# Second attention: queries and keys staged from ScalarE's queue instead of SyncE's

## The reference, cut to what matters

```python
q = qkv[..., :2 * Hx].reshape(Bx, 2 * NQ, Sx, HD)
k = qkv[..., 2 * Hx:2 * Hx + G].reshape(Bx, NKV, Sx, HD)
...
scores = jnp.einsum('bhqd,bhkd->bhqk', q, k) / math.sqrt(HD)
scores = jnp.where(causal, scores, -jnp.inf)
aw = jax.nn.softmax(scores, axis=-1)
...
aw = aw[:, :, 0] - lam * aw[:, :, 1]
attn = jnp.einsum('bhqk,bhkd->bhqd', aw, v) * (1.0 - LAMBDA_INIT)
```

## Time and profile before

| | |
|---|---|
| median of 3 runs | 695.55 us (694.66 to 696.96) |
| profiled execution, its own time | 693.89 us |
| its span, first to last instruction | 692.1 us |
| loop of the second attention | about 243 to 493 us |
| busy over the span: PE, DVE, ACT, POOL | 524.8, 469.4, 305.6, 341.8 us |
| mean granted clock of PE | 0.844 of full speed |

### The profile page before, as it was taken

The page is one execution under the profiler, slowest core; times in us unless marked ns, Lnnn a source line. Parts: engine busy times, 40 slices in busy tenths (PEclk is TensorE's granted clock), DMA queues, the critical chain, the costliest instruction groups (busy, mean ns, idle before and its releaser), DMA issues. The chain is left out here.

```text
span 692.1 us, 12597 instructions
## 1 busy us (share of the span) xinstructions
PE 524.8 (76%) x3770; PEld 352.6 (51%) x3770; DVE 469.4 (68%) x1716; ACT 305.6 (44%) x498; POOL 341.8 (49%) x489
## 2 busy tenths in 40 slices
PE   6686363987046799999899899999816189999950
PEld 3336262987023234544344444444416179999950
DVE  5958855554483897989799979995675734544535
ACT  3213011543016136767577667778411044445422
POOL 2050323777364425655467646855431067777622
PEclk9798855999558558999899989999965589999985
DMA  5000430111216434455654434433065011111122
GB/s 193 0 1 0 186 150 19 52 55 47 68 31 127 90 90 98 104 112 111 137 138 122 111 91 110 97 71 71 21 235 144 1 43 47 51 50 50 47 92 110
DMA packets 87891, 58.39 MB, mean 84 GB/s; under 512 B 72465, under 2 KB 73490, under 8 KB 85938
## 3 DMA queue, kind: packets, MB, share of 16 engines
q1 hardware_dynamic: 79826, 42.11, 24.3%
q0 software_dynamic: 3968, 8.13, 4.2%
q10 hardware_dynamic: 4032, 7.34, 3.0%
HBM read 37.93 MB, written 19.63 MB: 83 GB/s over the span
## 5 line engine op out<-in xcount | busy, mean ns | idle before, releaser
L1315 DVE CUSTOM_DVE_ANT_1 banks<-banks,a_mask 128x480 f32<-128x480 f32 (+14 forms) x480 | 189.8, 458 | 22.9 <-PE banks L1528 20.8
L1438 ACT ACTIVATE a_prob_<-banks 128x1024 f32<-128x1024 f32 x160 | 155.4, 1022 | 61.6 <-PE banks L1542 61.6
L1204 POOL TENSOR_SCALAR_AFFINE_SELECT a_prob_<-a_prob_ 128x512 f32<-128x512 f32 x128 | 81.2, 637 | 92.4 <-ACT a_prob_ L1438 91.4
L1528 PE MATMUL banks<-a_k_u_,a_q_u_ 72*128 72x512 bf16 (+15 forms) x512 | 108.9, 308 | 7.7 <-DVE a_neg_max_ L1315 4.8
L1542 PE MATMUL banks<-a_q_u_,a_k_x_ 75*128 75x512 bf16 x320 | 102.8, 403 | 7.1 <-DMA a_q_u_<-scratch_m_rows 6.3
L1528 PEld LDWEIGHTS banks<-a_k_u_,a_q_u_ 72*128 72x128 bf16 x512 | 64.9, 148 | 77.5 <-DVE a_neg_max_ L1315 41.0
L873 PE MATMUL banks<-f_hgt,f_w_now 128*112 128x128 f32 (+1 forms) x808 | 103.2, 280 | 0.4 <-DVE f_w_now L687 0.2
L873 PEld LDWEIGHTS banks<-f_hgt,f_w_now 128*112 128x112 f32 (+1 forms) x808 | 96.6, 186 | 1.2 <-DVE f_w_now L687 0.4
L540 POOL DMA_INDIRECT f_hg<-scratch_h_rows,f_source x62 | 60.2, 971 | 67.0 <-DVE f_home L676 48.1
L1554 PE MATMUL banks<-a_prob_,a_v_g_ 128*32 128x512 f32 (+3 forms) x1024 | 88.5, 466 | 0.0
L546 POOL DMA_INDIRECT scratch_back_rows<-f_y,f_home x62 | 61.2, 987 | 35.5 <-DVE f_y L713 26.3
(11 more groups left out here) (207 smaller groups left out, 677.5 us busy)
## 6 DMA issues: line engine op xcount, KB each, us to landing
a_q_u_<-scratch_q_parts SPq DMA_DIRECT2D x16, 576.0 KB
scratch_o_rows<-a_o_sb_ ACTq DMA_DIRECT2D x28, 256.0 KB, 3.1
w<-in_w SPq DMA_DIRECT2D x2, 2048.0 KB, 10.3
w<-in_w SPq DMA_DIRECT2D x2, 1792.0 KB, 10.0
scratch_q_parts<-a_part_ SPq DMA_DIRECT2D x24, 128.0 KB
a_k_u_<-scratch_k_parts SPq DMA_DIRECT2D x48, 48.0 KB
scratch_h_rows<-f_h SPq DMA_DIRECT2D x8, 256.0 KB, 5.6
f_back<-scratch_back_rows SPq DMA_DIRECT2D x4, 512.0 KB, 5.1
```

Of the source, the lines that this page charges most:

```text
L1204: nc.gpsimd.affine_select(out=block_p, in_=block_p, pattern=[[0, JH], [1, P]], compare_op=ALU.is_ge, fill=0.0, base=0, channel_multiplier= ...
L1315: last = nc.vector.tensor_tensor_reduce(out=found, in0=found, in1=mask[:, :, TG - 4 * (t + 1):], scale=-1.0, scalar=-MASKED, op0=ALU.add, ...
L1438: nc.scalar.activation(prob[g % 2][:, 2 * e:2 * e + 2].rearrange("p s j t c -> p (s j) t c"), PS[:, b0:b0 + 2, :].rearrange("p s (j c t) - ...
L1528: last = nc.tensor.matmul(PS[:, a % 3, off:off + width], queries[:, g % 2, :, t], k_u[r][:, :, g % 2 * TG:g % 2 * TG + 4 * (t + 1)], start ...
```

## The change

`stage` becomes a function of the queue that issues it and moves above the engines' blocks. SP still stages units 0, 1 and 2 ahead of the loop. Inside the loop the call goes from SP's even iterations to ACT's: behind the exponential e = 1 and, from g = 1 on, behind the copy of the outputs that follows it, and ahead of the exponential e = 2. The waits, the DMAs, their order and their semaphores are the same.

```diff
+        def stage(queue, u):
+            b, n, r = u // PER_B, u % PER_B, u % RING
+            queue.wait_ge(parts_out[b], 16 * PARTS_DMAS)
+            if u >= RING:
+                g = 2 * (u - RING) + 1
+                queue.wait_ge(score_mm, NE * (g + 1))
+                queue.wait_ge(cut_done, g + 1)
+            queue.dma_start(q_u[r][0:ROWS]...).then_inc(stage_in[r], 16)
+            for a in range(PARTS):
+                rows = slice(a * PARTS * HD, (a + 1) * PARTS * HD)
+                queue.dma_start(k_u[r][rows]...).then_inc(stage_in[r], 16)
...
             for b in range(2):
                 for n in range(PARTS):
                     write_part(b, n)
-                stage(b)
+                stage(sp, b)
...
-            stage(2)
+            stage(sp, 2)
             for g in range(GROUPS):
-                if g % 2 == 0 and g // 2 + RING - 1 < UNITS:
-                    stage(g // 2 + RING - 1)
                 if g + 1 < GROUPS:
                     maxima_in(g + 1)
...
                     exponentials(g, e)
                     if e == 1 and g >= 1:
                         copy_outputs(g - 1)
+                    if e == 1 and g % 2 == 0 and g // 2 + RING - 1 < UNITS:
+                        stage(ac, g // 2 + RING - 1)
                     if e == 2 and 1 <= g <= GROUPS - LATE:
                         outputs(g - 1)
```

More of the change, by code:

```diff
@@ L1014, in loads @@
             return g // 2 + 1
+        def stage(queue, u):
[5 more added lines that the diff above has]
+                queue.wait_ge(cut_done, g + 1)
+            queue.dma_start(q_u[r][0:ROWS].rearrange("r g c j t -> r (g c j t)"),
+                         dram["q_parts"][b, :, :, n].rearrange("a d g c t -> (a d) (g c t)").unsqueeze(1)
+                         .to_broadcast([PARTS * HD, PARTS, CQ * 2 * TG])).then_inc(stage_in[r], 16)
+            for a in range(PARTS):
+                rows = slice(a * PARTS * HD, (a + 1) * PARTS * HD)
+                queue.dma_start(k_u[r][rows].rearrange("r c t -> r (c t)"),
+                             dram["k_parts"][b, :, :, n].rearrange("a d c t -> d a (c t)")).then_inc(stage_in[r], 16)
         def heads(b):
@@ L1051, in write_part @@
                     sp.dma_start(dram["v_rows"][b].rearrange("(i p) d -> p i d", p=P), v_sb[b % 2][:]).then_inc(parts_out[b], 16)
[L1053 to L1067, removed]
             v_src = dram["v_rows"].rearrange("b t (c d) -> (b t c) d", d=HD).rearrange("(g k p) d -> g p k d", k=NQ, p=P)
```

## The result

The change makes the kernel slower: 707.6 us in the median of 5 runs (705.84 to 716.4), against 695.55 us (691.55 to 696.96) beside it. The ratio is 1.019, 95% interval 1.014 to 1.024. The whole changed kernel was measured a second time in another session, at 714.5 us in the median of six (704.8 to 718.66), against 691.43. The ratio there, 1.0246 [1.0184, 1.0309], leaves out three slow executions that lie over 1.5% above the fastest; the other three have a median of 708.11 us. The forecast was 710.5 us, with a range of 692 to 724.

A forecast was written before the change was run, and what follows sets the result against it. The prediction took a chain through PE, ACT and POOL, 7.06 us per iteration, to bound the kernel. Issue 13.8 + clock 13.6 - gain 12.4 = +15.0 us, making the median of 695.55 us 710.5, range 692 to 724.

The forecast's parts named there:

- The direction and the path: Slower (chance 0.77): staging on ACT delays exponential (g,2), then `scores(g,4)`, lengthening even iterations; PE's idle lets its clock fall.
- The threshold of 1.83 us: ACT, copy's start to exponential (g,2) plus cover: four issues under 0.76 + 1.07 us together never make `scores(g,4)` late.
- The issue on ACT: Staging's 2.90 us of issue ahead of exponential (g,2) costs 1.15 us in each of 12 even iterations, 13.8 us.
- The rival of the cheap issue: On ACT: four issues take under 1.83 us, nothing is late, the clock holds; 683 us, chance 0.15.
- The clock: PE idles 0.92 us ahead of `scores(g,4)` in even iterations; its clock falls 9 of 12 times, 1.51 us each, 13.6 us.
- the forecast's own range: Whole kernel: 704 to 716 us, with PE's clock falling in 5 to 12 of the even iterations.
- The rival of the held clock: On PE: idle stretches of 0.92 us may be too short to drop the clock; 697.0 us, chance 0.14.
- The gain: SP's maxima load no longer stands behind the staging; the excess of three long iterations, 12.4 us, is all gained.
- the chain of the 7.06 us: PE's `scores(g,4)`, ACT's fifth exponential, POOL's mask, then PE again: sets the length of an undisturbed iteration, 7.06 us.
- The forecast of +15.0: Whole kernel: 13.8 (issue) + 13.6 (clock) - 12.4 (gain) = +15.0 us, the median becoming 710.5 us.
- The rival of exclusion: ACT and SP exclude each other while issuing; SP's 0.51 us maxima store adds 12 x 0.5 = 6 us; 716.5 us, chance 0.05.

The follow-up runs named there:

- experiment 1: Changed kernel with ACT's staging split: queries behind exponential e = 0, first key DMA behind the output copy, others behind e = 3; 686.62 us against 693.08 before.
- Experiment 2: Changed kernel with only the third key DMA moved behind exponential e = 3, queries and two key DMAs kept ahead of e = 2; 694.06 us, ratio to before 1.001.
- experiment 3: Changed kernel with all three key DMAs moved behind exponential e = 3, only the query DMA kept behind the output copy; 689.59 us, ratio to before 0.9967.
- experiment 8: Changed kernel with PE repeating a row of maxima scores three times ahead of `scores(g,4)` in even iterations 2 to 24; 701.37 us, ratio to before 1.0104.
- experiment 5: Kernel before with the staging kept on SP but issued behind the loads of the next group's maxima and values; 684.96 us, ratio to before 0.9884.
- experiment 6: Kernel of experiment 5 without DVE's product with the coefficient in the factors, so outputs lack it; 679.46 us, one run, used only for its iterations.
- experiment 7: Kernel of experiment 5 with the factors' product moved from DVE to ACT behind e = 3, except the last batch; 709.49 us on another chip, ratio to before 0.9833.

## Why the prediction was right, and where it was not

**The direction and the path were right.** The threshold of 1.83 us is borne out: 2.91 us ahead of the exponential cost 1.2 us, 2.24 cost 0.5, 0.8 cost nothing there, and 2.9 in short pieces at three places cost nothing (experiments 1 to 3).

**The issue on ACT:** forecast 12 x 1.15 = 13.8 us; measured 12 x 1.2 = 14.5 (mean of the four held iterations 8.27, less 7.06). SP's rows were the right price. Over the whole trace of after, the two issuers of the query DMA stand side by side (shortest, median, longest ns):

```profile
L1024 ACTq DMA_DIRECT2D a_q_u_<-scratch_q_parts x13: 789/790/1372, 248.0 to 458.1; - x13
L1024 SPq DMA_DIRECT2D a_q_u_<-scratch_q_parts x3: 789/818/827, 219.1 to 248.8; - x3
```

The rival of the cheap issue fell with these rows. On the sentence of the Trainium skill that the issue is usually small relative to the DMA (DMA: Bandwidth & Descriptors, "Issuing engines are not separate DMA queues"): its main point, that a second issuing engine adds no DMA engines, agrees with these runs, since one queue reordered did as well as two; but the time of issue, 2.9 us of it, was not small here.

**The clock:** forecast 9 falls of 12 at 1.51 us, 13.6. Measured 8 in the first profile: the even iterations together lie 26.2 us above 12 x 7.06, 14.5 of it is the issue, which leaves 11.7, and the odd ones after a fall give 1.4 more (3, 5, 7, 9 and 11), 13.1 in all or 1.6 per fall. The second profile had 5 falls, below the 9, at the lower end of the 5 to 12 that the forecast's own range took. The size was right; that it varies by execution was in the range, not in the reasoning. The rival of the held clock came true for single stretches, 4 of 12 in the first profile and 7 of 12 in the second. That the falls come from the idle time, experiment 8 shows: take it away and there are none.

**The gain was mis-sized.** The one step that failed is "What is late next after such a wait goes is again the chain of the 7.06 us, so no more than the 12.4 comes back". I took all 12.4; by the iterations 11.05 came (experiment 5), by the medians 8.1. The late maxima had been hiding DVE's factors in iterations 11 and 19, and without them these take 8.12 where they took 7.33 and 7.34. I had read DVE's waits for PE, but not what DVE does once per batch. Experiments 6 and 7 show it. Against that, the iterations behind the long ones had carried some loss that I had not counted (before, all excess over 7.06 in 2 to 25 is 13.1 us, not 12.4).

**Iteration 1 was not foreseen.** It is worth +5.05 us in the profiled pair. The first profile of after has PE's clock at 0.50 in every window of 2 us from 262 to 276 (that of 272 to 274 is quoted above), where before has 0.50 from 262 to 264 and 0.89 already in the next. The second profile of the same kernel has 7.63 us there, and the kernel of 5 has 9.54. So it is no fixed effect of the change, and a good part of why this execution was the slowest of five.

**The sum** over the profiled pair, from the table of iterations: +14.5 (issue), +13.1 (falls), +5.05 (iteration 1), -13.1 (excess of before gone), +1.0 (factors in iteration 19) = +20.5 us, which is 252.52 - 231.99; 0.9 us came ahead of the first copy (264.33 against 263.45), and 1.2 lie behind. The medians differ by 12.05 us, so a middle execution of the first session must have had less of the two variable terms; that is argued, no profile of one was taken. The forecast of +15.0 lies between the first session's 12.05 and the second's, which is 16.7 by the three executions that its ratio takes (708.11 - 691.43) and 23.1 by all six. That it came so near is in part luck: two terms vary by execution, of which I had only one, and the gain was taken too high.

**The rival of exclusion** was 6 us in the even iterations. There it did not show: in iteration 14 SP stores its maxima at 378.45, inside ACT's three key DMAs (378.00, 2.11 us), and takes 0.36 us; in iteration 16, where SP issues nothing beside them, the three take 2.04. In iterations 10 and 18 SP's two gathers beside ACT's key DMAs take 1.52 and 1.49 us, against 1.23 in before, and ACT's take 2.08 and 2.06. That is some tenths of a us on SP, and none of the 0.5 on ACT. The last section has a longer pair.

**What stays open** is what decides, given PE's idle 0.9 us, whether the clock falls, and why iteration 1 starts at the low clock in some executions.

## What to carry to other kernels

A DMA's issue is work of the engine that issues it: before you move one to a "free" engine, add up the issue times of all its DMAs from the rows of the queue where they stand now, and ask what cover the next computation on the new engine has; issues of 0.7 to 0.8 us, each behind another instruction, left the iterations as they were, and one piece of 2.9 us cost 1.2 us each time. If the aim is that a small urgent load shall not stand behind large ones, put it ahead of them in the same queue first: this gave the whole gain here, and none of the loss. And before you count a removed wait as gained in full, look for what other engines did in it, above all work that comes once in many iterations: here DVE's factors.

## What the hardware showed unexpectedly

**Some long issues take a microsecond more.** Experiment 2, iteration 10, first ACT's queue, then SP's:

```profile
330.28 2.38 ACTq L1032 DMA_DIRECT2D a_k_u_<-scratch_k_parts  x2
```

```profile
331.13 2.42 SPq L1107 DMA_DIRECT2D a_o_b_<-scratch_o_rows  x2
```

ACT's two key DMAs take 2.38 us, against 1.35 to 1.41 in other iterations, and SP's two gathers beside them 2.42, against 1.23 with no neighbour. PE idled 1.24 us, and that iteration took 10.18 us. The Trainium skill (Perfetto Trace Analysis, "DMA Instruction — HWDGE (DVE, Sync)") tells of a descriptor generator locked by one sequencer at a time; the pair of rows is what one would see of that. But other rows speak against it as the cause. The same neighbours in iteration 18 of this profile take 1.37 and 1.52 us, and in iteration 10 of experiment 1 SP's gathers take 1.23 across two key DMAs of ACT. And the same microsecond comes with no issue of ACT beside it, in SP's queue of the kernel of 6:

```profile
347.72 2.17 SPq L1116 DMA_DIRECT2D a_r_w_<-scratch_r_rows  x2
```

One of these two takes 1.55 us, against 0.53 to 0.60 in before; in the profile of experiment 1 one of the same pair takes 1.69, again with nothing from ACT beside it. So what makes an issue longer now and then stays open; iteration 10 here is 2.6 us longer than the other even ones of 7.59, in part by the clock behind it (a pair of score matmuls at 335.61 takes 0.90 us, against 0.61).

**The same loop starts at either clock.** Iteration 1 took 7.05 to 7.63 us in eight profiles (both of before among them), 9.54 in one, and 12.60 to 12.65 in three. Those three have the staging on ACT in one piece, and so has one of the eight, so a part of the change in it is neither shown nor excluded. 5 us of 700 is more than the kernels of experiments 2 and 3 differ from before (1.0 and 1.8 us), so comparisons of one execution with one can't tell such edits; iteration lengths can.
